# Top-1 experts: outputs scattered to their tokens by carried row numbers, loaded back in order

## The chip, the cores and the metric

The kernel runs as one program on 1 core of a Trainium2 chip. The metric is the device time of one execution in microseconds (us), lower is better. A core has five engines that run side by side and meet at semaphores: TensorE (PE; its weight loads are shown as PEld), VectorE (DVE), ScalarE (ACT), GpSimd (POOL) and SyncE (SP, used here to issue transfers). 16 DMA engines move data between DRAM and the on-chip memory SBUF. Two ways of issuing a transfer matter here: SP issues plain ones, whose rows stand as `SPq DMA_DIRECT2D`; POOL issues the indirect ones, whose addresses come from a table of row numbers in SBUF, and stands as busy for the `DMA_INDIRECT` while it does so.

## The reference

Four transformer-like layers of 4096 tokens by 128 channels run in sequence, each as "x = x + mixer(norm(x))" and "x = x + feed-forward(norm(x))". The change is in the feed-forward of the second layer (L1), a mixture of 8 experts:

```python
def _L1_ffn_ref(x, router_w, W1, b1, W2, b2):
    ...
    capacity = int(math.ceil(T / E * CAPACITY_FACTOR))      # 4096 / 8 * 1.25 = 640
    logits = tokens @ router_w.T
    # top-1 expert; the tokens of an expert beyond its capacity (by probability) go to expert 0
    final_e = _route(tokens, router_w)
    out = jnp.zeros_like(tokens)
    for e in range(E):
        h = jax.nn.relu(tokens @ W1[e] + b1[e])             # 128 -> 512
        y = h @ W2[e] + b2[e]                               # 512 -> 128
        out = out + jnp.where((final_e == e)[:, None], y, 0.0)
    return out.reshape(Lx, Bx, D)
```

The other layers (two attentions, two gated mixtures, two state-space mixers, a spiking network) are not touched.

## The kernel before, in words

`build` calls the stages one after the other; each stage is a block in which the five engines have their own instruction lists, and at its end all engines meet before the next begins. The activations stand transposed in SBUF (`g.xT`, channels by tokens). `P` is 128, `TOK` 4096, `NT` = 32 tiles of 128 tokens, `CH` 512 and `NCH` = 8 chunks. Around the change the order is: `norm_stage` n3, `top1_stage` (routing), `expert_stage`, `norm_stage` n4.

**Routing (`top1_stage`).** PE makes the logits (L771). DVE takes the first maximum and the probability, then searches each expert's capacity threshold in 28 bisection steps, each with a count that PE sums over the partitions (L1010). Meanwhile PE turns the tokens' rows back (L998) and ACT copies them to `routed.rows` (L1123), 128 floats for each token. After the search DVE works out for each token a slot (`routed.slot`, L1099): the slots are grouped by expert and padded to blocks of 256 slots, 23 blocks (`BLOCKS`), 5888 slots (`SLOTS`) in all. After it come nine more instructions of DVE (L1101 to L1115), one after the other: which expert owns which block (`routed.expert`), and the biases of each block (`routed.b1`, `routed.b2`). POOL clears a 128x128 tile (L984), and SP writes it over the whole table `sent` in DRAM (L989), so that empty slots hold zeros.

**Experts (`expert_stage`).** POOL's list in order: 32 indirect scatters, one for each tile of 128 tokens, from `routed.rows` to the slots in `sent` (L1158); for each block two copies of its expert's weights to a ring of three buffers (L1164, L1165), the fourth and later ones after the block three back has been through both its matmuls (`y_ready`); at last a wait for all stores, and 32 indirect gathers (L1169), one for each tile of tokens, from `back` at the tokens' slots. SP's list: after all scatters have landed, 8 loads of `sent`, three blocks each (L1176), the next stage's weights (L83), and for each block a store of its output rows to `back`, in slot order (L1181). PE runs a software pipeline over the blocks: `turn_x(i+1)` (L1191), `up(i)` (L1200), `down(i-1)` (L1209), `turn_y(i-2)` (L1218). ACT does the four ReLUs of a block (L1252) and the copy of its output rows `rows(i)` to the ring `yr` of three (L1245), three blocks behind. DVE copies the turned inputs (L1265) and adds the second bias (L1271). Behind the last block PE turns each gathered chunk of four tiles (L1236) and DVE adds it to `g.xT` (L1282).

Of the kernel before, what the change touches and what calls it, by code (L numbers as in the profile page):

```python
# [18 lines left out]
P = 128  # L19
# [921 lines left out]
SLOTS = BLOCKS * BLOCK  # L941

class Routed:

    def __init__(self, nc, ctx):
        make = lambda n, shape, dt=F32: ctx.enter_context(nc.sbuf_tensor("f1_" + n, shape, dt))
        self.rows, self.slot = make("rows", [P, NT, P]), make("slot", [P, NT], mybir.dt.int32)
        self.expert = make("expert", [P, BLOCKS], mybir.dt.int32)  # L950
        self.b1, self.b2 = make("b1c", [P, BLOCKS, 4]), make("b2c", [P, BLOCKS])
# [4 lines left out]
def top1_stage(nc, g, name, w, experts, routed):  # L956
# [5 lines left out]
    with Stage(nc, name) as s:  # L962
# [4 lines left out]
        zero = s.sb("zero", [P, P])  # L967
        count_k, block_k = s.sb("count_k", [P, BLOCKS]), s.sb("block_k", [P, BLOCKS])
        own = s.sb("own", [P, BLOCKS, e])
        need, ends, expert = s.sb("need", [P, e]), s.sb("last", [P, e]), s.sb("expert", [P, BLOCKS])  # L970
        over, b1m, b2m = s.sb("over", [P, e, 16]), s.sb("b1m", [P, BLOCKS, 4, e]), s.sb("b2m", [P, BLOCKS, e])
# [9 lines left out]
        with nc.Block() as block:  # L981
            @block.gpsimd
            def _(pool):
                pool.memset(zero[:, :], 0.0).then_inc(zeroed, 1)  # L984

            @block.sync
            def _(sp):
                sp.wait_ge(zeroed, 1)
                sp.dma_start(routed.sent.rearrange("(i p) d -> p i d", p=P),  # L989
                             zero[:, :].unsqueeze(1).to_broadcast([P, SLOTS // P, P])).then_inc(cleared, 16)  # L990
# [3 lines left out]
            def _(pe):  # L994
# [26 lines left out]
            def _(dve):  # L1021
# [19 lines left out]
                link(dve.tensor_tensor(pm[:, :, :], oh[:, :, :], p1[:, :].unsqueeze(2).to_broadcast(wide), ALU.mult))  # L1041
                link(dve.memset(thr[:, :], 0.0))
# [57 lines left out]
                per_block = lambda t: t.unsqueeze(2).to_broadcast([P, BLOCKS, e])  # L1100
                link(dve.tensor_tensor(own[:, :, :], per_block(block_k[:, :]),  # L1101
# [1117 lines left out]
```

## Time and profile before

| | |
|---|---|
| median of 3 runs | 3723.78 us (3715.41 to 3729.06) |
| the profiled execution's own time | 3735.14 us, span 3733.4 us |
| mean granted TensorE clock | 0.877 of full speed |
| busy share of the span: PE, DVE, ACT, POOL | 79%, 68%, 49%, 19% |
| routing stage, first to last work | 2159.2 to 2277.9 us |
| experts, 32 scatters on POOL | 2279.1 to 2319.3 us |
| experts, 23 blocks | 2324.0 to 2417.7 us |
| experts, 32 gathers, turns and adds | 2420.3 to 2463.5 us |
| norm stage n4 begins | 2465.6 us |

A row of a timeline reads: start, duration, engine, line, operation, output<-inputs, shapes, count, and in brackets how long the engine had been idle before it and what ended the idle time. A row of the windows reads: stretch, its length, then the busy time and number of instructions of PE, PEld, DVE, ACT and POOL, then the granted clock of TensorE (1.00 is 2.4 GHz, 0.50 is 1.2 GHz), the busy share of the DMA engines and the GB/s that they moved.

### The profile page before, as it was taken

To read this page: it belongs to the slowest core of one execution; us is meant where nothing else is said; L and a number is where in the kernel's file an instruction comes from. 1 tells how busy PE (TensorE), PEld (TensorE's weight loads), DVE (VectorE), ACT (ScalarE), POOL (GpSimd) and SP (SyncE) were. 2 spreads that over 40 slices of the span, in tenths; PEclk is the share of its full clock that TensorE was granted. 3 is DMA by queue.
4 is the path that set the end of the run, shared out by engine and by line. 5 is a ranking of instruction groups with operands and counts; after the bars stand their busy time and mean duration, and the time that the engine had idled before them with its cause. 6 is when DMAs were issued, how large, how long until landed. Compare 5 with 4: busy or idle time off the path is not lost. (4 is left out here: it accounts for less than half of the span.)

```text
span 3733.4 us, 43485 instructions
## 1 busy us (share of the span) xinstructions
PE 2943.2 (79%) x12844; PEld 1022.8 (27%) x12844; DVE 2552.6 (68%) x2898; ACT 1818.1 (49%) x3121; POOL 726.6 (19%) x820
## 2 busy tenths in 40 slices
PE   6499999975999948999999542856777786996756
PEld 3122222213333321222222131722223333332322
DVE  4699999923444459999997252147999984447448
ACT  2288888851212226888888300425655541224333
POOL 3311111100000031111110003223777760000000
PEclk8599999965999968999999655977999997998778
DMA  3210111002000040010100212110100000001010
GB/s 118 81 27 23 27 27 26 23 20 68 0 0 0 0 156 22 23 27 22 27 22 19 97 34 58 36 46 23 42 6 12 12 1 0 0 0 56 0 45 23
DMA packets 113619, 116.36 MB, mean 31 GB/s; under 512 B 37118, under 2 KB 89982, under 8 KB 113100
## 3 DMA queue, kind: packets, MB, share of 16 engines
q1 hardware_dynamic: 99148, 84.38, 7.6%
q0 software_dynamic: 14336, 30.44, 2.8%
q8 instruction: 53, 0.87, 0.1%
q14 instruction: 82, 0.67, 0.1%
HBM read 64.15 MB, written 50.59 MB: 31 GB/s over the span
## 5 line engine op out<-in xcount | busy, mean ns | idle before, releaser
L640 DVE TENSOR_REDUCE a_att_mx<-a_att_s 128x2 f32<-128x1024 f32 x1024 | 1205.3, 1220 | 104.1 <-PE a_att_s L551 91.9
L625 ACT ACTIVATE a_att_pt<-a_att_st 128x512 f32<-128x512 f32 x2048 | 1064.7, 602 | 283.0 <-PE a_att_st L577 265.0
L577 PE MATMUL a_att_st<-a_att_qst,a_att_kst 50*128 50x512 bf16 x2048 | 636.1, 394 | 75.4 <-ACT a_att_pt L625 62.7
L551 PE MATMUL a_att_s<-a_att_kst,a_att_qst 50*128 50x512 bf16 x2048 | 531.7, 402 | 83.9 <-DMA a_att_kst<-a_kstk 50.9
L564 PE MATMUL a_att_av<-a_att_pt,a_att_vst 128*32 128x512 f32 x4096 | 565.9, 626 | 0.0
L577 PEld LDWEIGHTS a_att_st<-a_att_qst,a_att_kst 50*128 50x128 bf16 x2048 | 158.3, 94 | 766.1 <-ACT a_att_pt L625 708.3
L929 DVE TENSOR_TENSOR f_h<-f_sg,f_up 128x512 f32<-128x512 f32 x184 | 126.6, 688 | 309.4 <-ACT f_sg L917 309.4
L917 ACT ACTIVATE f_sg<-f_gp 128x512 f32<-128x512 f32 x184 | 109.9, 597 | 461.2 <-PE f_cp L906 461.2
L1656 POOL TENSOR_TENSOR g_xn<-m2s_hs,m2s_cb 128x1024 f32<-128x1024 f32 x128 | 300.8, 2354 | 119.0 <-DVE m2s_hs L1623 62.2
L1623 DVE TENSOR_TENSOR_SCAN m2s_hs<-m2s_da,m2s_bps 128x1024 f32<-128x1024 f32 x128 | 292.7, 2287 | 4.4
L1539 PE MATMUL m2s_yps<-g_xn,g_ident 128*128 128x512 f32 x512 | 242.8, 597 | 0.9
L487 POOL CAST a_att_mt_in<-a_att_nmax 128x16 bf16<-128x16 f32 x64 | 12.6, 196 | 1081.3 <-DVE a_att_nmax L648 1081.3
L1595 ACT COPY m2s_cb<-m2s_cps 128x1024 f32<-128x1024 f32 x128 | 129.5, 1012 | 183.9 <-POOL g_xn L1656 182.4
L551 PEld LDWEIGHTS a_att_s<-a_att_kst,a_att_qst 50*128 50x128 bf16 x2048 | 113.4, 94 | 237.9 <-DVE a_att_mx L640 168.5
L163 POOL MEMSET n_mean_w<- 128x128 f32 x8 | 1.6, 204 | 898.6 <-POOLq L875 586.8
L1618 DVE TENSOR_TENSOR m2s_bps<-m2s_dtx,m2s_bps 128x1024 f32<-128x1024 f32 x128 | 154.8, 1209 | 3.8 <-POOL m2s_dtx L1642 3.8
L1590 ACT ACTIVATE m2s_da<-m_dt,m2s_aneg 128x1024 f32<-128x1024 f32 x128 | 147.4, 1151 | 0.0
L1559 PE MATMUL m2s_bps<-m_bcs,m2s_sel 96*128 96x512 bf16 x256 | 79.2, 392 | 85.5 <-DVE m2s_hs L1623 82.7
L931 DVE TENSOR_TENSOR f_h<-f_h,f_cp 128x512 f32<-128x512 f32 x184 | 126.4, 687 | 6.3
L896 PE MATMUL f_yp<-f_h,area 128*128 128x512 f32 x224 | 126.0, 645 | 4.3 <-DVE f_h L931 4.3
L270 ACT ACT_TABLE_LOAD x9 | 11.5, 1283 | 224.3 <-PEq L696 107.7
L1539 PEld LDWEIGHTS m2s_yps<-g_xn,g_ident 128*128 128x128 f32 x512 | 97.1, 191 | 85.2 <-issue 63.9
(387 smaller groups left out, 3590.1 us busy)
## 6 DMA issues: line engine op xcount, KB each, us to landing
a_att_qst<-a_qstk POOLq DMA_DIRECT2D x128, 100.0 KB, 2.5
a_att_kst<-a_kstk POOLq DMA_DIRECT2D x128, 100.0 KB, 2.5
a_qstk<-a_qkv_part SPq DMA_DIRECT2D x96, 128.0 KB, 1.9
a_kstk<-a_qkv_part SPq DMA_DIRECT2D x96, 128.0 KB, 2.0
a_num<-a_att_oev SPq DMA_DIRECT2D x256, 16.0 KB
a_out_nm<-a_num SPq DMA_DIRECT2D x16, 256.0 KB, 3.4
a_out_rb<-a_rden SPq DMA_DIRECT2D x16, 256.0 KB, 4.5
area<-in_f_w_dram SPq DMA_DIRECT2D x2, 2048.0 KB, 10.1
```

Of the source, the lines that this page charges most:

```text
L551: mm = pe.matmul(s1[:, cut % 2, h, :], qst[u][64 * h:64 * h + STACK, qt * P:(qt + 1) * P], kst[u][64 * h:64 * h + STACK, kh * CH:(kh + 1) ...
L564: mm = pe.matmul(av[32 * gr:32 * gr + 32, :], vst[u][:, kt, h, :], pt[:, 4 * (kt % 4) + 2 * half + h, :], start=kt == 0, stop=kt == 7)
L577: pe.matmul(st[:, e % 3, :], kst[u][64 * h:64 * h + STACK, kt * P:(kt + 1) * P], qst[u][64 * h:64 * h + STACK, half * CH:(half + 1) * CH], ...
L625: act.activation(pt[:, e % 16, :], st[:, e % 3, :], ACT.Exp, scale=scale).then_inc(exp_done, 1)
L640: dve.tensor_reduce(mx[:, par, 2 * cut:2 * cut + 2], s1[:, cut % 2, :, :], AX.X, ALU.max).then_inc(s1_used, 1)
L929: dve.tensor_tensor(h1[:, j % 2, :], sg[:, j % 2, :], up[:, j % 2, :], ALU.mult).then_inc(h1_done, 1)
L1539: mm = pe.matmul(yps[:, f, :], g.ident[:, :], hc[:, k % 4, f * CH:(f + 1) * CH], start=n == 0, stop=n == NS - 1)
L1590: act.activation(da[:, k % 4, :], dt[:, q % 2, span(q)], ACT.Exp, scale=aneg[:, q % 2, n:n + 1]).then_inc(da_done, 1)
L1595: act.copy(cb[:, k % 2, :], both(cps[:, :, :])).then_inc(c_copied, 1)
L1618: dve.tensor_tensor(over, dtx[:, q % 2, :], over, ALU.mult).then_inc(dbx_done, 1)
L1623: dve.tensor_tensor_scan(hs[:, k % 3, :], da[:, k % 4, :], over, 0.0, ALU.mult, ALU.add).then_inc(scan_done, 1)
L1656: pool.tensor_tensor(hc[:, k % 4, :], hs[:, k % 3, :], cb[:, k % 2, :], ALU.mult).then_inc(hc_done, 1)
```

## The change

The rows that travel get wider: 132 floats (`WIDE`) in place of 128, where the float at place 128 holds a number. For a token's row it is the token's own number; for every row of the cleared table it is 4096 plus the slot's number. So after the scatter each slot carries the row of `back` to which its output belongs, and `back` grows to 4096 + 5888 rows. In `top1_stage` this takes one matmul, five small DVE instructions ahead of the search, a larger memset on POOL (128x6072 in place of 128x128), and a clearing transfer that waits for the numbers. In `expert_stage` DVE turns the numbers of three blocks to integers at a time (`take_numbers`, 8 times), and POOL, for each block, issues two indirect scatters of its 256 output rows straight to their tokens' rows; SP then has no stores in the loop, and at the end loads the 4096 rows in order with 8 plain transfers. The 32 gathers are gone. The nine DVE instructions that make the blocks' experts and biases stand at the head of `expert_stage`; POOL's weight copies and ACT's first ReLU wait for them (`blocks_ready`). The weight ring has four buffers in place of three, and ACT's `rows` runs two blocks behind in place of three.

```diff
@@ Routed
-        self.rows, self.slot = make("rows", [P, NT, P]), make("slot", [P, NT], mybir.dt.int32)
+        self.rows, self.slot = make("rows", [P, NT, WIDE]), make("slot", [P, NT], mybir.dt.int32)
-        self.sent = nc.dram_tensor("f1_sent", [SLOTS, P], F32, kind="Internal").ap()
-        self.back = nc.dram_tensor("f1_back", [SLOTS, P], F32, kind="Internal").ap()
+        self.sent = nc.dram_tensor("f1_sent", [SLOTS, WIDE], F32, kind="Internal").ap()
+        self.back = nc.dram_tensor("f1_back", [TOK + SLOTS, P], F32, kind="Internal").ap()
@@ top1_stage, POOL and SP
-                pool.memset(zero[:, :], 0.0).then_inc(zeroed, 1)
+                pool.memset(empty[:, :, :], 0.0).then_inc(zeroed, 1)
+                pool.memset(routed.rows[:, :, P:WIDE], 0.0).then_inc(zeroed, 1)
-                sp.wait_ge(zeroed, 1)
-                sp.dma_start(routed.sent.rearrange("(i p) d -> p i d", p=P),
-                             zero[:, :].unsqueeze(1).to_broadcast([P, SLOTS // P, P])).then_inc(cleared, 16)
+                sp.wait_ge(zeroed, 2)
+                sp.wait_ge(numbered, 1)
+                sp.dma_start(routed.sent.rearrange("(i p) d -> p i d", p=P), empty[:, :, :]).then_inc(cleared, 16)
@@ top1_stage, PE (behind the logits) and DVE (ahead of the search)
+                pe.matmul(pre_ps[:, 0:1], before_w[:, :], g.ones[:, 0:1], start=True, stop=True).then_inc(place_ps_ready, 1)
+                dve.wait_ge(place_ps_ready, 1)
+                link(dve.tensor_scalar(serial[:, :], g.ones[:, 0:SLOTS // P], float(P), None, ALU.mult))
+                link(dve.tensor_tensor_scan(number[:, :], g.ones[:, 0:SLOTS // P], serial[:, :], -float(P), ALU.mult, ALU.add))
+                link(dve.tensor_tensor(number[:, :], number[:, :], pre_ps[:, 0:1].to_broadcast([P, SLOTS // P]), ALU.add))
+                dve.wait_ge(zeroed, 2)
+                link(dve.tensor_copy(routed.rows[:, :, P], number[:, 0:NT]))
+                dve.tensor_scalar(empty[:, :, P], number[:, :], float(TOK), None, ALU.add).then_inc(numbered, 1)
@@ top1_stage, DVE: L1100 to L1115 leave; they stand at the head of expert_stage's DVE list, the last with
+                dve.tensor_reduce(routed.b2[:, :], b2m[:, :, :], AX.X, ALU.add).then_inc(blocks_ready, 1)
+                dve.wait_ge(blocks_ready, 1)
@@ expert_stage, POOL
                 pool.wait_ge(w.here, w.all)
+                pool.wait_ge(blocks_ready, 1)
+
+                def take_weights(i):
+                    first = pool.value_load(routed.expert[0:1, i:i + 1], min_val=0, max_val=7) * CH
+                    if i >= 4:
+                        pool.wait_ge(y_ready, i - 3)
+                    pool.tensor_copy(wu[:, i % 4, :], w1[:, bass.ds(first, CH)]).then_inc(w_copied, 1)
+                    pool.tensor_copy(wd[:, i % 4, :], w2[:, bass.ds(first, CH)]).then_inc(w_copied, 1)
+
+                for i in range(4):
+                    take_weights(i)
                 for i in range(BLOCKS):
-                    first = pool.value_load(routed.expert[0:1, i:i + 1], min_val=0, max_val=7) * CH
-                    if i >= 3:
-                        pool.wait_ge(y_ready, i - 2)
-                    pool.tensor_copy(wu[:, i % 3, :], w1[:, bass.ds(first, CH)]).then_inc(w_copied, 1)
-                    pool.tensor_copy(wd[:, i % 3, :], w2[:, bass.ds(first, CH)]).then_inc(w_copied, 1)
-                for u in range(3):
-                    pool.wait_ge(r_stored[u], 16 * len(range(u, BLOCKS, 3)))
-                for t in range(NT):
-                    pool.indirect_dma_start(got[:, t, :], None, routed.back, place(t)).then_inc(gathered[t // 4], 16)
+                    if i + 4 < BLOCKS:
+                        take_weights(i + 4)
+                    if i % 3 == 0:
+                        pool.wait_ge(to_ready, i // 3 + 1)
+                    pool.wait_ge(r_copied, i + 1)
+                    for j in range(wide):
+                        pool.indirect_dma_start(routed.back, bass.IndirectOffsetOnAxis(
+                            ap=to[:, wide * i + j:wide * i + j + 1], axis=0), yr[:, i % 3, j, :], None).then_inc(r_sent[i % 3], 16)
@@ expert_stage, SP
-                for i in range(BLOCKS):
-                    sp.wait_ge(r_copied, i + 1)
-                    sp.dma_start(back[:, wide * i:wide * (i + 1), :], yr[:, i % 3, :, :]).then_inc(r_stored[i % 3], 16)
+                for u in range(3):
+                    sp.wait_ge(r_sent[u], 32 * len(range(u, BLOCKS, 3)))
+                for c in range(NCH):
+                    sp.dma_start(got[:, 4 * c:4 * c + 4, :], back[:, 4 * c:4 * c + 4, :]).then_inc(got_here[c], 16)
@@ expert_stage, PE
-                    pe.wait_ge(gathered[c], 64)
+                    pe.wait_ge(got_here[c], 16)
@@ expert_stage, ACT
-                        act.wait_ge(r_stored[i % 3], 16 * (i // 3))
+                        act.wait_ge(r_sent[i % 3], 32 * (i // 3))
+                act.wait_ge(blocks_ready, 1)
-                    if i >= 3:
-                        rows(i - 3)
-                for i in range(BLOCKS - 3, BLOCKS):
+                    if i >= 2:
+                        rows(i - 2)
+                for i in range(BLOCKS - 2, BLOCKS):
                     rows(i)
@@ expert_stage, DVE
+                def take_numbers(k):
+                    dve.wait_ge(x_here[k], 16)
+                    part = slice(wide * groups[k][0], wide * (groups[k][-1] + 1))
+                    dve.tensor_copy(to[:, part], xs[:, part, P]).then_inc(to_ready, 1)
+                    if i % 3 == 0 and i < BLOCKS:
+                        take_numbers(i // 3)
```

## Rows read from the trace of the kernel before

**Rows 1.** Windows of the expert stage and the norm stage behind it: busy time, clock, DMA share.

```profile
2320.60:2333.00 12.40, 8.95 (x36) 7.37 (x37) 2.04 (x5) 3.36 (x8) 2.72 (x6) 0.70 1.01 265
2332.00:2410.00 78.00, 78.00 (x402) 68.72 (x401) 17.30 (x41) 38.58 (x99) 23.38 (x40) 1.00 0.12 35
2426.60:2463.50 36.90, 8.93 (x32) 5.73 (x32) 5.50 (x8) 0.00 (x0) 25.47 (x27) 0.50 0.19 50
2465.50:2471.00 5.50, 5.18 (x6) 2.19 (x7) 1.38 (x2) 2.75 (x4) 1.09 (x2) 0.50 0.00 0
```

**Rows 2.** Timeline of VectorE at the end of the routing stage (start us, us).

```profile
2272.96 0.18 DVE L1099 CAST f_slot<-f1r_tmp 128x32 int32<-128x32 f32 x1
2273.17 0.35 DVE L1101 TENSOR_TENSOR f1r_own<-f1r_block_k,f1r_last 128x184 f32<-128x184 f32 x1
...
2274.75 1.41 DVE L1109 TENSOR_TENSOR f1r_b1m<-f1r_own,area 128x736 f32<-128x736 f32 x1
...
2277.53 0.34 DVE L1115 TENSOR_REDUCE f_b2c<-f1r_b2m 128x23 f32<-128x184 f32 x1
```

**Rows 3.** Timelines, VectorE and GpSimd: the nearest rows for the added small operations.

```profile
2178.59 0.18 DVE L1045 TENSOR_SCALAR f1r_count_k<-f1r_block_k 128x23 f32<-128x23 f32 x1
...
2134.61 0.95 POOL L164 MEMSET n_inv<- 128x1024 f32 x1
```

**Rows 4.** Timeline of GpSimd: first and last of 32 scatters, then the weight copies.

```profile
2279.09 1.06 POOL L1158 DMA_INDIRECT f_sent<-f_rows,f_slot  x1 [119.69 <-POOLq L981]
...
2318.34 0.96 POOL L1158 DMA_INDIRECT f_sent<-f_rows,f_slot  x1 [0.30 <-issue]
...
2319.31 0.62 POOL L1164 COPY f_wu<-area 128x512 f32 x1
```

**Rows 5.** One line's instructions: duration in ns, min/median/max, of the GpSimd DMAs.

```profile
L1158 POOL DMA_INDIRECT f_sent<-f_rows,f_slot x32: 954/958/1061, 2279.1 to 2318.3; - x32
...
L1169 POOL DMA_INDIRECT f_got<-f_back,f_slot x32: 940/944/1001, 2420.3 to 2459.1; - x32
...
L478 POOL DMA_DIRECT2D a_att_qst<-a_qstk x128: 518/518/738, 129.9 to 2005.4; - x128
```

**Rows 6.** Timeline of one block in the steady part of the block loop.

```profile
2367.18 0.61 POOL L1164 COPY f_wu<-area 128x512 f32 x1 [2.72 <-PE f_yp L1209]
...
2368.35 1.70 ACT L1252 ACTIVATE f_h<-f_zp,f_b1c 128x256 f32<-128x256 f32 x4 [1.93 <-PE f_zp L1200]
...
2370.74 0.38 PE L1218 MATMUL f_rp<-g_ident,f_y 128*128 128x128 f32 x2
```

**Rows 7.** Timeline from the last blocks to the first work of the next stage.

```profile
2413.76 0.37 ACT L1245 COPY f_yr<-f_rp 128x256 f32<-128x256 f32 x1 [0.84 <-PE f_rp L1218]
2417.31 0.37 ACT L1245 COPY f_yr<-f_rp 128x256 f32<-128x256 f32 x1 [0.59 <-PE f_rp L1218]
...
2420.30 1.00 POOL L1169 DMA_INDIRECT f_got<-f_back,f_slot  x1 [13.03 <-DMA f_back<-f_yr]
2426.67 1.11 PE L1236 MATMUL f_zp<-g_ident,f_got 128*128 128x128 f32 x4 [9.40 <-DMA f_got<-f_back,f_slot]
2462.79 0.69 DVE L1282 TENSOR_TENSOR g_xT<-g_xT,f_zp 128x512 f32<-128x512 f32 x1 [4.22 <-PE f_zp L1236]
2465.56 0.20 POOL L163 MEMSET n_mean_w<- 128x128 f32 x1 [5.55 <-POOLq L1153]
```

**Rows 8.** First loads; landing of the gathers, then of the clearing transfer; POOL's DMA queue.

```profile
2320.59 7.68 SPq L1176 DMA_DIRECT2D f_xs<-f_sent  x8
...
2323.96 1.12 PE L1191 MATMUL f_xp<-g_ident,f_xs 128*128 128x128 f32 x4 [56.26 <-DMA f_xs<-f_sent]
...
DMA to landing us min/median/max: 2.4/2.5/2.6
...
DMA to landing us min/median/max: 11.8/11.8/11.8
...
q0 software_dynamic: 2048, 4.20, 7.3%
```

More of the change, by code:

```diff
@@ L966, in top1_stage @@
         thr, cand, part, inc = (s.sb(x, [P, e]) for x in ("thr", "cand", "part", "inc"))
[L967 to L971, printed above, removed]
+        empty = s.sb("empty", [P, SLOTS // P, WIDE])
+        serial, number = s.sb("serial", [P, SLOTS // P]), s.sb("number", [P, SLOTS // P])
+        place_ps_ready, numbered = s.sem("place_ps_ready"), s.sem("numbered")
+        count_k = s.sb("count_k", [P, BLOCKS])
+        need, ends, block_k = s.sb("need", [P, e]), routed.ends, routed.block_k
+        over = s.sb("over", [P, e, 16])
         ps = s.ps("ps", [P, NT * e])
@@ L1099, in _ @@
                 link(dve.tensor_copy(routed.slot[:, :], tmp[:, :]))
-                per_block = lambda t: t.unsqueeze(2).to_broadcast([P, BLOCKS, e])
-                link(dve.tensor_tensor(own[:, :, :], per_block(block_k[:, :]),
-                                       ends[:, :].unsqueeze(1).to_broadcast([P, BLOCKS, e]), ALU.is_ge))
-                link(dve.tensor_reduce(expert[:, :], own[:, :, :], AX.X, ALU.add))
-                link(dve.tensor_scalar(expert[:, :], expert[:, :], float(e - 1), None, ALU.min))
-                link(dve.tensor_copy(routed.expert[:, :], expert[:, :]))
-                link(dve.tensor_tensor(own[:, :, :], per_block(expert[:, :]),
-                                       block_k[:, 0:e].unsqueeze(1).to_broadcast([P, BLOCKS, e]), ALU.is_equal))
-                dve.wait_ge(experts.here, experts.all)
-                link(dve.tensor_tensor(b1m[:, :, :, :], own[:, :, :].unsqueeze(2).to_broadcast([P, BLOCKS, 4, e]),
-                                       experts.tiles["b1"].rearrange("p (e t) -> p t e", t=4).unsqueeze(1).to_broadcast(
-                                           [P, BLOCKS, 4, e]), ALU.mult))
-                link(dve.tensor_reduce(routed.b1[:, :, :], b1m[:, :, :, :], AX.X, ALU.add))
-                link(dve.tensor_tensor(b2m[:, :, :], own[:, :, :],
-                                       experts.tiles["b2"].unsqueeze(1).to_broadcast([P, BLOCKS, e]), ALU.mult))
-                link(dve.tensor_reduce(routed.b2[:, :], b2m[:, :, :], AX.X, ALU.add))
             @block.scalar
@@ L1122, in _ @@
                     act.wait_ge(turned, c + 1)
-                    act.copy(routed.rows[:, 4 * c:4 * c + 4, :],
+                    act.copy(routed.rows[:, 4 * c:4 * c + 4, 0:P],
                              tps[:, c % 4, :].rearrange("p (t d) -> p t d", d=P)).then_inc(copied, 1)
@@ L1137, in expert_stage @@
         got = s.sb("got", [P, NT, P])
-        wu, wd = s.sb("wu", [P, 3, CH]), s.sb("wd", [P, 3, CH])
+        own, expert = s.sb("own", [P, BLOCKS, 8]), s.sb("number", [P, BLOCKS])
+        b1m, b2m = s.sb("b1m", [P, BLOCKS, 4, 8]), s.sb("b2m", [P, BLOCKS, 8])
+        step, blocks_ready = s.sem("step"), s.sem("blocks_ready")
+        wu, wd = s.sb("wu", [P, 4, CH]), s.sb("wd", [P, 4, CH])
         w_copied = s.sem("w_copied")
@@ L1146, in expert_stage @@
         r_turned, r_copied = s.sem("r_turned"), s.sem("r_copied")
-        r_stored = [s.sem(f"r_stored{u}") for u in range(3)]
-        gathered = [kept(f"gathered{c}") for c in range(NCH)]
+        to_ready, r_sent = s.sem("to_ready"), [kept(f"r_sent{u}") for u in range(3)]
+        got_here = [s.sem(f"got_here{c}") for c in range(NCH)]
         o_turned, o_added = s.sem("o_turned"), s.sem("o_added")
         sent = routed.sent.rearrange("(i p) d -> p i d", p=P)
-        back = routed.back.rearrange("(i p) d -> p i d", p=P)
+        back = routed.back[0:TOK, :].rearrange("(t p) d -> p t d", p=P)
         at = lambda i: (slice((i % 2) * BLOCK, (i % 2 + 1) * BLOCK))
```

34 lines of the change are left out of this document (28 added, 6 removed).

## The prediction

> **What bounds the kernel now.** The kernel is a chain of stages that do not overlap, so I first cut the expert stage into stretches and ask of each what ends it. I read four views: the windows, to see which engine fills a stretch; the timelines of VectorE and GpSimd, to see what stands alone; the durations of the GpSimd transfers; and the timeline of the last blocks. The windows [rows 1] show two quite different halves. In the block loop TensorE is busy 78.00 of 78 us at a granted clock of 1.00, so no other engine's work costs anything there as long as it fits under TensorE. From 2426.6 to 2463.5 us TensorE is busy 8.9 of 36.9 us, VectorE 5.5, and GpSimd 25.5: here the 32 gathers are the path. GpSimd's timeline [rows 4] shows that the 32 scatters in front are a path of the same kind: from 2279.09 to 2318.34 us is 31 steps, 1.266 us each, 0.96 of it the instruction and 0.30 the idle time before it. Between the routing's last instruction and the first scatter VectorE runs nine instructions on which the scatters do not depend [rows 2].
>
> **The change, part by part.**
>
> *The routing's end.* The slots are ready at 2272.96 + 0.18. The nine instructions from 2273.17 to 2277.53 + 0.34 leave the path: −4.70 us. They run beside the scatters instead, which take 40 us, and who waits for them (the weight copies, the first ReLU) comes behind the scatters; their cover is eight times their size. If the cover failed, the price is the same 4.7 us.
>
> *The numbers, ahead of the search.* Five small VectorE instructions on 46 or 32 columns. The nearest row is the 0.18 us one on 23 columns [rows 3]; with the gap to the next in the chain I take 0.24 us, 1.2 us together. Bounds are 1.0 and, by the 0.35 us of the 184 columns in [rows 2], 1.9 us. The extra matmul stands behind the logits, and TensorE's next wait there is on VectorE's first count, behind the same five instructions: nothing. GpSimd's memset grows to 6072 columns: by 0.95 us for 1024 [rows 3] 5.6 us, from 2159 to 2165; VectorE asks for it at 2178 (the row of L1045 is what now follows these instructions): nothing. The clearing transfer starts at about 2180 instead of 2160 and landed 11.8 us after its issue (the second landing line of [rows 8]); the stage ends 80 us later: nothing.
>
> *The 32 scatters with wider rows.* 528 bytes a row for 512. The queue moved 4.20 MB in 2048 packets [rows 8]: 64 indirect transfers of 128 rows are 8192 rows, so four rows of 512 bytes to a packet, and no sign of a limit at one row's size. The count of rows is unchanged; I take 1.266 us as before. Bounds: nothing, and 3.3 us if each took the slowest of 1061 ns [rows 5].
>
> *The first load.* It landed 3.4 us after its issue (2320.59 to 2323.96) [rows 8]; 3% more bytes are nothing. The four weight copies in front of the loop (4.5 us by two of some 0.6 each) end at about 2323.8, but the first block's pair is done at 2320.4: nothing. 
> *The block loop.* The period is 2.72 us idle plus two copies, 3.89 us [rows 6]. GpSimd gets two scatters for each block: 2 x 1.26 = 2.52, with the copies 1.17, together 3.69 us of 3.89. It fits by 0.2 us, which is thin, so I also ask what happens if it does not. The scatters are behind everything TensorE needs: the weight ring of four and the row ring of three give TensorE more than 3 us of lag before it stalls. What counts is the end of GpSimd's chain. The first rows are ready near 2336.3 (2414.13 less 20 periods); from there 46 scatters and 18 pairs of copies are 58.0 + 21.1 us, to 2415.4, while the rows of the last block are only ready at 2417.68. So in the loop nothing is lost. ACT's `rows(i-2)` now waits for the `turn_y` of the same round, which ends at 2370.74 + 0.38 = 2371.12; the copy takes 0.37 us [rows 7], to about 2371.6, and the next ReLU starts a period after 2368.35, at 2372.24 [rows 6]: 0.6 us of room, nothing. Its wait for `r_sent` is for rows scattered three periods (11.7 us) ago; those need 2.5 us of issue and 2.5 to land: nothing. The eight number casts are about 0.2 us of VectorE, which is busy 17.3 of 78 us: nothing.
>
> *The end.* Before, from the last rows at 2417.31 + 0.37 = 2417.68 to the last add's end at 2462.79 + 0.69 = 2463.48: 45.8 us [rows 7]. After, by steps. Block 20's rows are ready at 2413.76 + 0.37 = 2414.13; three blocks of scatters follow back to back, 7.6 us, to 2421.7. The last one lands 2.5 us after its start at 2420.7 (the landing that the gathers show, 2.4 to 2.6 [rows 8]): 2423.2. The first plain load, 256 KB against the 384 KB that took 3.4 us: 2.9 us, and 0.1 for the issue: 2426.2. The eight chunks: the loads come at 265 GB/s [rows 1], 1.0 us each, and TensorE turns a chunk in 1.11 us at a clock of 0.50 [rows 7], so TensorE sets the pace: 8 x 1.12 = 9.0, to 2435.2. The last add: 0.7 us, 2435.9. That is 18.2 us in place of 45.8: −27.6 us. The bounds: if the clock rises in the dense turns the loads pace them, −1.0; and n4, whose first 5.5 us ran at 0.50 [rows 1], could start at full clock, at most half of that, −2.7. The other way, a slower landing and loads without overlap with the turns: +3.
>
> *Sum.* −4.7 + 1.2 − 27.6 = −31.1 us. Against the profiled execution's own 3735.14 us it gives 3704.0; that execution was 11.4 us above the median, and I take the same difference from the median: 3723.78 − 31.1 = **3692.7 us**, 0.8% less. What this measurement can tell from no change is about 0.5%, 18.6 us.
>
> **The rivals.**
>
> *VectorE holds up the scatters (−26 to −29 us).* Nine instructions now run while GpSimd writes its transfers. In the profile the scatters ran while VectorE was idle. For the rival: nothing measured beside it. Against: attention's GpSimd transfers, made while every engine works, keep 518 ns in the median of 128, 738 at worst [rows 5], and the 32 gathers, beside the turns and adds, stayed at 940 to 1001 ns [rows 5]. Its price is at most the nine instructions, 4.7 us, giving 3697.4. The Trainium skill ("SBUF — State Buffer", Summary: rules for kernel authors) says that a VectorE instruction that uses both its ports, or has two SBUF inputs against a GpSimd one that reads SBUF, fully blocks the other. By it the two-input instructions (1.41 [rows 2] and three of some 0.35) and two small copies could cost up to 2.8 us, 3695.5; inside the loop VectorE reads PSUM, and that page has no block there.
>
> *GpSimd becomes the bound of the loop (slower than before).* In the loop the scatters would have to take longer than alone. The chain has 6.3 us of room (2415.4 to 2421.7). At 1.5 us a scatter the chain is 46 x 0.24 = 11.0 us longer, and the end moves by 4.7: 3697.4. The gain is gone when one takes 1.26 + (6.3 + 31.1)/46 = 2.07 us, 64% more; at 2.5 us the kernel is 20 us slower, 3743. For it: 3.69 of 3.89 us is thin, and no indirect transfer of the profile ran beside a busy TensorE and ScalarE. Against: the attention rows above, and the worst of 32 scatters at 1.06.
>
> *The wider row costs a second piece (no change).* If 528 bytes were issued as 512 and 16, the instruction's 0.96 us could double: 32 x 0.96 = 30.7 us, and the sum is −0.4: 3723. The packets of four rows speak against it.
>
> *The end is longer than thought (−20 to −26 us).* Eight loads behind a wait for 46 scattered writes, whose landing to DRAM rows spread at random no row shows; with 3 us more for landing and 4 for loads one after the other, 3700.
>
> **Chances and range.** Forecast, −28 to −36 us: 0.66. A smaller gain by one of the rivals above, −19 to −28: 0.22. Nothing left, by the second piece or by both thin places: 0.07. GpSimd as the bound and slower: 0.05. Faster by over 0.5%: 0.88, within: 0.07, slower: 0.05. The low end: −31.1 − 3.7 for the clock, less 5 for the scatter of medians of few runs, 3684. The high end: −31.1 + 4.7 + 3.3 + 0.7 = −22.4, and 5 for the same: 3706. What lies beyond is 0.15.
>
> **What would show it.** After: no `DMA_INDIRECT` that writes `got`; VectorE's block work between the first and fourth scatter; the stage's first scatter 3.5 us closer to the routing's start; 32 scatters in 40 us; a TensorE busy all through 23 periods of 3.89 us; the last output scatter 4 us behind the last copy of rows; and 18 us from there to the last add. Wrong it would be if scatters in the loop take over 1.4 us, if the period of the loop leaves 3.89, if the first 32 stretch, or if the eight loads come much slower than 1.1 us apiece.

## The result, and the profile after

The changed kernel took 3687.4 us in the median of six executions, the kernel before 3724.56 us in six beside them: a ratio of 0.9887, 95% interval [0.9866, 0.9908]. On 3724.6 us that is 42 us less, between 34 and 50. Timed twice more beside the kernel before, the same file came out at 0.9901 [0.9877, 0.9925] and 0.9914 [0.9887, 0.9940]. The mean of all 24 executions is 3688.7 us, that of the 81 of the kernel before 3725.2 us: 36.5 us less, 1.0%. Forecast were 31.1 us less and a range from 3684 to 3706. The six executions' median lies inside it; the first ratio, taken of the 3723.78 us from which the range was worked out, gives 3681.7 us, 2 us below it.

The profiled execution took 3684.66 us, its span is 3683.3 us. Laid beside the profile before, by stages (us; the norm stages' starts are GpSimd's memset of L163):

| stretch | before | after | change |
|---|---|---|---|
| first norm stage to second (first attention, untouched) | 861.6 | 842.9 | −18.7 |
| second norm stage to routing (untouched) | 1284.1 | 1283.6 | −0.5 |
| routing, to the first input scatter | 119.9 | 116.2 | −3.7 |
| first input scatter to last | 39.25 | 40.10 | +0.85 |
| last input scatter to first turn of a block | 5.6 | 5.8 | +0.2 |
| first turn to last rows | 93.7 | 94.9 | +1.2 |
| last rows to last add | 45.8 | 16.8 | −29.0 |
| last add to next stage | 2.1 | 0.5 | −1.6 |
| norm stage n4 | 24.7 | 21.9 | −2.8 |
| n4's end to the end (untouched) | 1243.1 | 1247.0 | +3.9 |

The touched stages and n4 give 34.8 us. What else differs lies in code that the change does not touch, and there is a theory to test.

Windows of the changed kernel (stretch, length, busy time of PE, PEld, DVE, ACT, POOL, then the granted clock, DMA share and GB/s):

```profile
2298.70:2311.00 12.30, 8.66 (x28) 6.97 (x29) 1.28 (x4) 3.35 (x8) 3.12 (x6) 0.60 1.07 272
2311.00:2389.00 78.00, 78.00 (x401) 68.75 (x401) 17.69 (x47) 40.59 (x99) 58.79 (x76) 1.00 0.10 33
...
2414.40:2420.00 5.60, 5.31 (x12) 2.20 (x12) 3.43 (x5) 4.01 (x6) 1.09 (x2) 1.00 0.00 0
```

These answer to [rows 1]. TensorE is again busy 78.00 of 78 us in the loop, and GpSimd there went from 23.4 to 58.8 us without costing TensorE anything. In the last row n4's first 5.6 us run at a clock of 1.00; before it was 0.50.

The timelines of VectorE and of GpSimd around the stage's start, to lay beside [rows 2, 4]:

```profile
2254.87 0.18 DVE L1112 CAST f_slot<-f1r_tmp 128x32 int32<-128x32 f32 x1
2255.56 0.35 DVE L1282 TENSOR_TENSOR f_own<-f_block_k,f_ends 128x184 f32<-128x184 f32 x1 [0.51 <-PEq L985]
...
2256.75 0.35 DVE L1287 TENSOR_TENSOR f_own<-f_number,f_block_k 128x184 f32<-128x184 f32 x1
2257.14 1.42 DVE L1290 TENSOR_TENSOR f_b1m<-f_own,area 128x736 f32<-128x736 f32 x1
2258.59 0.92 DVE L1293 TENSOR_REDUCE f_b1c<-f_b1m 128x92 f32<-128x736 f32 x1
```

```profile
2256.28 1.05 POOL L1158 DMA_INDIRECT f_sent<-f_rows,f_slot  x1 [110.92 <-POOLq L985]
2257.63 1.78 POOL L1158 DMA_INDIRECT f_sent<-f_rows,f_slot  x1 [0.30 <-issue]
2259.72 1.00 POOL L1158 DMA_INDIRECT f_sent<-f_rows,f_slot  x1 [0.30 <-issue]
...
2296.38 0.95 POOL L1158 DMA_INDIRECT f_sent<-f_rows,f_slot  x1 [0.30 <-issue]
```

The slots are ready at 2255.05, the block work stands at 2255.56 behind the stage's switch, and the first scatter issues 1.2 us behind the slots. The second scatter takes 1.78 us in place of 0.96. It starts 0.5 us into VectorE's 1.42 us instruction with two inputs and ends 0.85 us behind it. The first, with the 0.35 us two-input instruction at 2256.75 wholly inside it, takes 1.05 us, as before (1.06).

GpSimd in the steady loop, the first scatter of four blocks in a row, with the number cast and the copy of rows that the fourth of them needs:

```profile
2362.83 0.16 DVE L1315 CAST f_to<-f_xs 128x6 int32<-128x6 f32 x1
2363.40 0.97 POOL L1178 DMA_INDIRECT f_back<-f_yr,f_to  x1 [0.97 <-DVE f_to L1315]
...
2366.98 0.97 POOL L1178 DMA_INDIRECT f_back<-f_yr,f_to  x1 [0.17 <-issue]
...
2370.71 0.96 POOL L1178 DMA_INDIRECT f_back<-f_yr,f_to  x1 [0.33 <-ACT f_yr L1256]
...
2373.95 0.37 ACT L1256 COPY f_yr<-f_rp 128x256 f32<-128x256 f32 x1 [1.11 <-PE f_rp L1229]
2375.08 0.96 POOL L1178 DMA_INDIRECT f_back<-f_yr,f_to  x1 [0.97 <-DVE f_to L1315]
```

Three blocks in 11.68 us, 3.893 each: TensorE's period. From 2363.40 to 2366.98 GpSimd runs free, at 3.58 us a block; then it catches up with the rows and waits for them, 0.33 us and 0.97 us. The profile puts the 0.97 us down to a number cast, but the cast that this block needs had ended 12 us before. The block waits for its rows too: they stood at 2374.32, and it starts 0.76 us behind them, where the block before starts 0.28 us behind its own. Why each third block, the one that also asks for its numbers, starts later is not shown. GpSimd's scatters take 954/963/972 ns (min/median/max of 46).

The end, to lay beside [rows 7]:

```profile
2396.75 0.37 ACT L1256 COPY f_yr<-f_rp 128x256 f32<-128x256 f32 x1 [0.59 <-PE f_rp L1229]
...
2400.70 0.96 POOL L1178 DMA_INDIRECT f_back<-f_yr,f_to  x1 [0.30 <-issue]
2402.98 5.37 SPq L1192 DMA_DIRECT2D f_got<-f_back  x8
...
2405.90 1.97 PE L1247 MATMUL f_zp<-g_ident,f_got 128*128 128x128 f32 x8 [9.19 <-DMA f_got<-f_back]
...
2410.38 3.54 DVE L1327 TENSOR_TENSOR g_xT<-g_xT,f_zp 128x512 f32<-128x512 f32 x5 [0.18 <-PE f_zp L1247]
...
2414.43 0.20 POOL L163 MEMSET n_mean_w<- 128x128 f32 x1 [12.78 <-POOLq L1153]
```

The last scatter ends 4.5 us behind the last rows, the loads issue 1.3 us later, the first turn comes 2.9 us behind the issue, and the last add ends 8.0 us after that, at 2413.92. The steps forecast were 4.0, 1.6, 2.9 and 9.7. The first is 0.5 us longer because the last three blocks do not follow back to back: block 21's rows stood at 2396.15, and its first scatter began at 2396.91.

### The profile page after: what moved, and what is told of

It is laid out like the page before. It is cut to its first block and busy times, and to the rows that moved or that the text cites. A ratio compares the mean times of both kernels' runs of the same rounds, so it can differ in the third digit from the quotient of the medians.

```text
span 3683.3 us, 43526 instructions
## 1 busy us (share of the span) xinstructions
PE 2919.2 (79%) x12846; PEld 1023.0 (28%) x12846; DVE 2553.5 (69%) x2911; ACT 1819.9 (49%) x3121; POOL 746.6 (20%) x835
## 5 line engine op out<-in xcount | busy, mean ns | idle before, releaser
L564 PE MATMUL a_att_av<-a_att_pt,a_att_vst 128*32 128x512 f32 x4096 | 554.1, 614 | 0.0
L163 POOL MEMSET n_mean_w<- 128x128 f32 x8 | 1.6, 204 | 896.8 <-POOLq L875 586.5
L904 PE MATMUL f_gp<-g_xn,area 128*128 x224 | 115.8, 599 | 4.3 <-POOL f_sel L884 4.3
```

The source lines that it names most:

```text
L564: mm = pe.matmul(av[32 * gr:32 * gr + 32, :], vst[u][:, kt, h, :], pt[:, 4 * (kt % 4) + 2 * half + h, :], start=kt == 0, stop=kt == 7)
```

## The experiments

**Is the part outside the stages real?** The kernel before against itself, and the changed kernel twice more. No edit.

> The kernel before, unchanged, timed against itself. Theory A (the 19 us by which the first attention was shorter in the profile after, with no edit in it, are the scatter of single executions): a ratio of 1.000 with an interval of some 0.003, and a first attention (from the first norm stage's start at 13.5 us to the second's) that lies anywhere from 843 to 862 us. Rival B (something in the changed program makes the untouched stages faster): the first attention again at 862 us here.

Measured: ratio 1.0003 [0.9982, 1.0023], twelve executions from 3712 to 3744. Its timeline has the norm stages' starts here:

```profile
13.64 0.20 POOL L163 MEMSET n_mean_w<- 128x128 f32 x1 [10.66 <-POOLq L101]
...
858.16 0.20 POOL L163 MEMSET n_mean_w<- 128x128 f32 x1 [93.40 <-POOLq L696]
```

and the changed kernel's is

```profile
13.65 0.20 POOL L163 MEMSET n_mean_w<- 128x128 f32 x1 [10.77 <-POOLq L101]
...
856.50 0.20 POOL L163 MEMSET n_mean_w<- 128x128 f32 x1 [92.95 <-POOLq L696]
```

The kernel before can do the first attention in 844.5 us too. Over the 15 profiles of this study it took 841 to 845 us in eight and 861 us in five, two times 852, in kernels of both kinds; the second attention took 845 to 848 us in thirteen and 864 to 865 in two. The length changes from one execution of the same file to the next. Theory A holds.

The traces also show where the 18 us lie. The end of the first attention in the profile before, in `before_warm`, in this run and in the changed kernel:

```profile
770.00:800.00 30.00, 27.20 (x102) 3.57 (x99) 0.00 (x0) 17.51 (x34) 0.00 (x0) 0.52 0.03 5
770.00:800.00 30.00, 25.66 (x129) 4.62 (x129) 0.00 (x0) 22.64 (x44) 0.00 (x0) 0.78 0.02 3
770.00:800.00 30.00, 23.61 (x150) 5.50 (x153) 0.00 (x0) 26.40 (x52) 0.00 (x0) 1.00 0.02 4
770.00:800.00 30.00, 24.09 (x157) 5.41 (x153) 0.00 (x0) 26.12 (x51) 0.00 (x0) 1.00 0.02 3
```

It is TensorE's granted clock: 1.00 in this stretch in the eight short ones, 0.50 to 0.52 in the five long ones, 0.78 and 0.79 in the two of 852 us. The two long second attentions have 0.69 in a stretch of 30 us near their end where the thirteen others have 1.00. From 760 to 770 us the clock stood at 1.00 with TensorE busy 8.40 of 10 us, in the profile before and in this run alike; then it fell in the one and not in the other. What made it fall is not shown.

> The changed kernel, unchanged, once more. Stage by stage the change should be worth 32.0 us from the routing's start to the next norm stage's and 2.8 us in that norm stage, 34.8 us or a ratio of 0.9907. Theory A: the ratio comes out at 0.990 to 0.992, and the first attention differs from the 842.9 us of the other profile. Rival B: the ratio is again 0.9887 or below, and the first attention is near 843 us.

Measured: 0.9901 [0.9877, 0.9925]; routing's start to n4's 275.4 us, n4 22.0, first attention 843.1. The stages gave 33.7 us this time. The ratio could be of either theory, so:

> The changed kernel a third time, unchanged. Theory A (the untouched attention stages have two lengths some 18 us apart, drawn anew in each execution, so that medians of few runs scatter by several us about the 34.8 us that the stages show): ratio between 0.989 and 0.993, nearer to 0.9907 than the first 0.9887. Rival B (a gain of some 7 us outside the stages that the change touches): 0.9885 or below.

Measured: 0.9914 [0.9887, 0.9940]; stages 275.2 and 21.0 us, 34.9 us less than before. By the ratio the gain outside did not come back. The three ratios centre on 0.9901, the stages say 0.9907.

**The block work undone.** L1100 to L1115 stand again at the end of the routing, and the waits for `blocks_ready` are gone:

```diff
@@ top1_stage, DVE
                 link(dve.tensor_copy(routed.slot[:, :], tmp[:, :]))
+                link(dve.tensor_tensor(own[:, :, :], per_block(block_k[:, :]), ...))
...
+                link(dve.tensor_reduce(routed.b2[:, :], b2m[:, :, :], AX.X, ALU.add))
@@ expert_stage, POOL and ACT
-                pool.wait_ge(blocks_ready, 1)
-                act.wait_ge(blocks_ready, 1)
```

> The changed kernel with one part undone: the nine VectorE instructions that make the blocks' experts and biases are back at the end of the routing, ahead of the scatters. The prediction's step (4.7 us off the path) says that from the routing's start to the next norm stage it takes 4.7 us more than the change as made, less the 0.8 us by which the second scatter was longer beside them, so 3.9 us more, and that the 32 scatters are back at 40.2 us. Rival (the move is worth nothing, since the scatters or the stage's switch hide it): 0 to 1 us more.

Measured: ratio 0.9915 [0.9890, 0.9940]. Routing to the first scatter took 121.1 us in place of 116.2, the scatters 39.24 in place of 40.10, and routing to n4 279.4 us: 4.0 to 5.1 us more than the changed kernel's three profiles (274.4 to 275.4). The second scatter took 0.97 us again. The step is right, with the long scatter as its price.

**More load on GpSimd in the loop.**

```diff
+                    for j in range(1):    # 2 in the second kernel; the waits on r_sent count them
+                        pool.indirect_dma_start(routed.spare, bass.IndirectOffsetOnAxis(
+                            ap=to[:, wide * i + j:wide * i + j + 1], axis=0), yr[:, i % 3, j, :], None).then_inc(r_sent[i % 3], 16)
```

> The changed kernel with one more indirect scatter per block in the loop, to a table that nobody reads (three in place of two); the output is unchanged. In the changed kernel's trace GpSimd's free period is 3.57 us (two scatters, two copies) under TensorE's 3.89. Theory (the prediction's chain: nothing is lost until GpSimd's chain is longer than TensorE's, and then its length counts alone): the period becomes 4.83 us for the 18 steps with a weight copy and 3.79 for the last four, the last scatter ends 105.7 us after the first in place of 85.0, and routing to next norm takes 20.7 us more than the change as made. Rival (TensorE stalls for weights or rows on top, and the two delays add): more than 25 us.

> The same with two more scatters per block (four in place of two). Theory: 6.09 us a block, 134.6 us from first to last, 49.6 us more than the change as made: slower than the kernel before by 15. The step from one extra to two is 23 x 1.26 = 29 us, each scatter at its full price once GpSimd is the bound. Rival (stalls add): more than 55 us.

Measured, routing to n4: 293.7 us with one more (19.3 us more than the changed kernel, forecast 20.7) and 324.1 us with two (49.8, forecast 49.6). The steady loop with one more:

```profile
2361.16 0.97 POOL L1179 DMA_INDIRECT f_back<-f_yr,f_to  x1 [0.17 <-issue]
...
2363.71 0.96 POOL L1182 DMA_INDIRECT f_spare<-f_yr,f_to  x1 [0.30 <-issue]
...
2366.01 0.97 POOL L1179 DMA_INDIRECT f_back<-f_yr,f_to  x1 [0.17 <-issue]
```

4.85 us a block and no wait but GpSimd's own issue. The two executions took 3705.7 and 3740.8 us. From the first output scatter to the end of the last it is 85.0 us in the changed kernel, 105.7 with one more a block and 134.7 with two, where 85.0, 105.7 and 134.6 were forecast. So the chain that the prediction used is the right model: the margin is spent first, about 8 us of it over the loop (23 x 1.26 less 20.7), and then each scatter costs its full 1.26 us, 23 times. Stalls of TensorE add nothing that shows. (The 1.4 us by which the first kernel came out below its forecast lie ahead of the chain: its first rows stood 12.4 us behind the first turn, the changed kernel's 13.8, with a clock of 1.00 against 0.70 in the second four us.)

**The scatters, but not under the loop.**

```diff
-y, yr = s.sb("y", [P, 2, BLOCK]), s.sb("yr", [P, 3, wide, P])
+y, yr = s.sb("y", [P, 2, BLOCK]), s.sb("yr", [P, BLOCKS, wide, P])
@@ POOL
+                for i in range(BLOCKS):
...
-                    pool.wait_ge(r_copied, i + 1)
+                    pool.wait_ge(r_copied, BLOCKS)
@@ ACT, rows(i)
-                        act.wait_ge(r_sent[i % 3], 32 * (i // 3))
```

> The changed kernel with the output scatters not block by block: GpSimd waits for the last block's rows and issues all 46 then, from a row buffer of 23 blocks. The output is unchanged. Theory (the change gains because the indirect transfers lie under TensorE's block loop; by themselves they are dearer than the 32 gathers): 46 x 1.266 = 58.2 us behind the last rows at about 2397.2, 53.8 us more than the change as made, about 19 us slower than the kernel before: ratio 1.005. Rival (it gains because plain loads in order replaced the gathers, whatever the place of the scatters): at most 10 us more than the change as made.

Measured: ratio 1.0022 [1.0007, 1.0038], slower than before. First and last of the 46:

```profile
2394.67 0.97 POOL L1179 DMA_INDIRECT f_back<-f_yr,f_to  x1 [15.06 <-ACT f_yr L1255]
...
2451.49 0.95 POOL L1179 DMA_INDIRECT f_back<-f_yr,f_to  x1 [0.30 <-issue]
```

56.8 us from start to start, 1.263 us each, and routing to n4 took 328.7 us: 54.3 more than the change as made. With n4's clock it is 19 us more than before by the stages; the ratio says 3 to 14. The direction is clear, the size is not the same in both. (The lowest of its ten executions, 3729.9 us, lies 20 us above the lowest of the 81 of the kernel before, 3709.9, which fits the stages.) Plain ordered loads alone do not make the gain. 46 scatters are dearer than 32 gathers, and they pay because they lie under TensorE.

**n4 and the clock.** Matmuls that nobody reads keep TensorE at work during the gathers of the kernel before:

```diff
+                def warm(n):
+                    for _ in range(n):
+                        pe.matmul(xp[:, 0, :], g.ones[:, :], g.xn[:, 0:CH], start=True, stop=True)
+
+                warm(8)                       # 10 in the second kernel
                 for c in range(NCH):
                     pe.wait_ge(gathered[c], 64)
...
                     mm.then_inc(o_turned, 1)
+                    if c < NCH - 1:
+                        warm(3)               # second kernel: 4, and 2 behind the last chunk
```

> The kernel before, with extra matmuls on TensorE whose result nobody reads: eight of 512 columns behind the block loop, and three behind each turned chunk but the last, so that TensorE stays busy while the gathers run. The output is unchanged. Theory (the 2.8 us that the norm stage behind gains come from TensorE's clock, which was still at 2.4 GHz when it began): the gathers take as long as before, the norm stage begins at a clock of 1.00 and takes 21.9 us in place of 24.7; 2.8 us faster in all, ratio 0.9992. Rival (the norm stage gains from something else in the change): it still takes 24.7 us.

Measured: ratio 0.9988 [0.9971, 1.0005], n4 24.6 us. It missed its condition, as the windows show, the second of them n4's start:

```profile
2420.00:2442.00 22.00, 13.03 (x41) 5.90 (x42) 2.75 (x4) 0.00 (x0) 16.51 (x19) 1.00 0.19 51
2450.73:2456.23 5.50, 5.24 (x6) 2.18 (x7) 1.38 (x2) 2.75 (x4) 1.09 (x2) 0.50 0.02 3
```

> The first such run missed its own condition: the clock had fallen to 0.50 before the norm stage began. Now the kernel before has ten extra matmuls of 512 columns behind the block loop, four behind each turned chunk and two behind the last. Theory (the 2.8 us of the norm stage are TensorE's clock): if the norm stage begins at a clock of 1.00 it takes 21.9 us in place of 24.7. Rival (it gains from something else): 24.7 us at a clock of 1.00.

Measured: the last extra matmul ended at 2442.45, TensorE then had 1.9 us without work, and n4 began at 2444.05 with a clock that fell in its first microseconds:

```profile
2442.00:2444.00 2.00, 0.45 (x2) 0.00 (x0) 0.00 (x0) 0.00 (x0) 0.00 (x0) 1.00 0.00 0
2444.05:2449.55 5.50, 5.24 (x9) 2.22 (x10) 2.04 (x3) 2.74 (x4) 1.09 (x2) 0.69 0.00 0
```

It took 23.7 us (the one execution, 3712.6). The condition was met by half, and so was the gain. Ordered by the mean clock of n4's first 5.5 us, over the 15 profiles: 0.50, 24.6 to 24.7 us (three profiles, all with gathers); 0.69, 23.7; 1.00, 21.0 to 22.0 (eleven). The length follows the clock, also within the kernel with the gathers. I take the term as TensorE's clock, shown in direction and, from one half-way point, in size.

**VectorE beside the input scatters.** Sixteen instructions that nobody needs, behind the block work:

```diff
                 dve.wait_ge(blocks_ready, 1)
+                for _ in range(16):
+                    link(dve.tensor_copy(got[:, 0:16, :].rearrange("p t d -> p (t d)"), g.xn[:, 0:2048]))
+                    # second kernel: dve.tensor_tensor(same, g.xn[:, 0:2048], g.xn[:, 2048:4096], ALU.add)
```

> The changed kernel with 16 more VectorE copies of 128x2048 float32 from SBUF to SBUF beside the 32 input scatters, behind the nine block instructions; nobody reads what they write. In the changed kernel the second of the 32 scatters took 1.78 us in place of 0.96, beside the 1.42 us two-input instruction and the two small copies. Theory A (the Trainium skill, SBUF page: a VectorE copy in a two-port mode and a GpSimd instruction exclude each other, descriptor writing too): the scatters beside the copies take up to a copy's length more each, and the 32 take 5 to 20 us more than 40.1. Rival B (the long scatter was of the two-input instruction's making or of chance): 40.1 us, and no scatter over 1.1 us but the one.

> The same with 16 VectorE additions of two SBUF inputs, 128x2048 float32 each, some 2.1 us apiece. Theory A (two SBUF inputs exclude a GpSimd instruction that reads SBUF; whether descriptor writing is one is what the page leaves as inferred): if it does, the scatters beside them stretch by 5 to 30 us in all; if only the two-port copies do, they stay at 40.1 us with one long one at the start. By the changed kernel's trace, where the long scatter lies under the 1.42 us two-input instruction, I expect them to stretch.

Measured, first input scatter to last: 50.1 us with the copies, 57.5 us with the additions, against 40.1. (The one execution of each took 3726.4 and 3694.1 us; both attentions were long in the first and neither in the second, so the totals say nothing of the scatters.) The copies (one merged row of 16) and one scatter beside and one behind them:

```profile
2295.28 20.37 DVE L1299 COPY f_got<-g_xn 128x2048 f32<-128x2048 f32 x16
...
2303.45 2.22 POOL L1158 DMA_INDIRECT f_sent<-f_rows,f_slot  x1 [0.30 <-issue]
...
2316.07 0.96 POOL L1158 DMA_INDIRECT f_sent<-f_rows,f_slot  x1 [0.31 <-issue]
```

and the additions with the same:

```profile
2256.51 37.19 DVE L1299 TENSOR_TENSOR f_got<-g_xn 128x2048 f32<-128x2048 f32 x16
...
2280.87 2.03 POOL L1158 DMA_INDIRECT f_sent<-f_rows,f_slot  x1 [0.30 <-issue]
...
2294.83 0.96 POOL L1158 DMA_INDIRECT f_sent<-f_rows,f_slot  x1 [0.30 <-issue]
```

**What the profile pointed to further.** TensorE starts the block loop at a clock of 0.60 (the first window of the changed kernel, shown above) and the search runs at 0.50. Extra matmuls in front of the loop, and in the second kernel in each step of the search too:

```diff
@@ expert_stage, PE (POOL counts its first 26 scatters on a semaphore of their own)
+                pe.wait_ge(early, 16 * 26)
+                for _ in range(8):
+                    pe.matmul(zp[:, 0, :], g.ones[:, :], g.xn[:, 0:CH], start=True, stop=True)
                 turn_x(0)
@@ top1_stage, PE, each step of the search (second kernel only)
                     turn(k + 3)
+                    for _ in range(2):
+                        pe.matmul(tot_ps[:, 0:256], g.ones[:, :], g.xn[:, 0:256], start=True, stop=True)
                     pe.wait_ge(counted_here, k + 1)
```

> The changed kernel with eight matmuls of 512 columns on TensorE, whose result nobody reads, placed so that they run while the last six input scatters go out (a semaphore of its own for the first 26). Theory (the first blocks ran at a clock of 0.50 after 47 us without work; the changed kernel still has this): the block loop starts at 1.00, the first three blocks take some 3 us less, from routing to next norm 271 us in place of 274.4; ratio to the kernel before 0.990. Rival (the clock falls again before the first block, or the loop's first steps wait for loads anyway): nothing.

> The same, and in each of the 29 steps of the threshold search two more matmuls of 256 columns on TensorE ahead of its wait for VectorE's count. Theory: at a clock of 1.00 the count that VectorE waits 0.69 us for each time comes about 0.2 us sooner, 29 times: the routing takes 110 to 112 us in place of 116.2, and with the 3 us above the whole is some 8 us faster than the changed kernel, ratio 0.988. Rival (the clock does not hold between so few columns, or the extra matmuls delay the count): 116 us or more.

Measured by stages: routing to n4 272.4 us with the first edit and 268.4 us with both, against 274.4 to 275.4: 2 to 3 and 6 to 7 us less (forecast were 3, and some 8). In the second the routing took 113.0 us for 110 to 112 forecast, the clock stood at 0.66 in the search and not at 1.00, and the loop began at 1.00:

```profile
2145.00:2252.00 107.00, 74.08 (x257) 52.52 (x257) 61.93 (x229) 4.99 (x9) 0.11 (x1) 0.66 0.12 29
2296.00:2304.00 8.00, 5.62 (x27) 4.21 (x26) 1.26 (x4) 2.80 (x7) 2.31 (x5) 1.00 1.10 282
```

The ratios are 0.9888 [0.9859, 0.9918] and 0.9907 [0.9874, 0.9939] (with one execution of 8436 us apart from the rest), which cannot be told from the changed kernel's. By stages the second is the fastest version here, 6 to 7 us ahead of the changed kernel and 4 ahead of the first edit; by the timing that is not shown.

## Why the prediction was off, point by point

The mechanism was right and the sum came close, 31.1 us for the 34.8 that the stages show; the low end of the range was wrong. The step that failed is the range's: "less 5 for the scatter of medians of few runs". The attention stages change by 18 us from one execution to the next, in both kernels, with TensorE's granted clock, and a ratio of six to twelve executions moves by more than 5 us: the same file gave 0.9887, 0.9901 and 0.9914, that is 42, 37 and 32 us less. The first lies 7 us beyond the 34.8 us of the stages, which alone would give 3689 us, inside the range. The three times shown spread by 13.6 us, and that could have been read as more than 5 on a median. The profile before held a sign too: the end of its first attention ran at a clock of 0.52 (shown above), and the end of its second, the same lines of the kernel, at 1.00:

```profile
2036.68:2066.68 30.00, 24.16 (x157) 5.57 (x153) 4.60 (x6) 26.46 (x52) 0.41 (x2) 1.00 0.04 7
```

The sum was 3.7 us short of the stages' gain. It had no term for the stage's switch (1.6 us), and it left n4's clock (2.8 us) out as a bound.

The terms, forecast and measured in the first profile:

- *The routing's end*, −4.7 + 1.2 = −3.5: −3.7, and the undoing of the move cost 4 to 5 us. Right.
- *The numbers, the clearing transfer, the memset*: the five instructions took 1.1 us (forecast 1.2), the rest nothing, as said; the memset took 5.16 us (forecast 5.6).
- *The scatters with wider rows*: 0.96 us as before. The second piece for 528 bytes, and with it the rival of no change, is gone.
- *VectorE holds up the scatters*: this rival came true at a sixth of its bound, +0.85 us. The evidence used against it did not bear on it: attention's transfers, which are plain ones, ran beside reductions, and the gathers beside adds of which one input is PSUM. Neither made them longer.
- *The first load*: 5.8 us from the last scatter to the first turn against 5.6. The Trainium skill's rule ("DMA: Bandwidth & Descriptors", How a descriptor splits into AXI transactions), by which the prediction estimated 0.4 us, is neither borne out nor refuted: no run here tells 0.4 from this 0.2.
- *The block loop*: no loss to GpSimd, as said, with 3.58 us free a block (forecast 3.69). From the first turn to the last rows it took 1.2 us more, at a clock of 0.60 where before it was 0.70 in the stretch around the first blocks; this was not forecast. Over the profiles without extra scatters this length, too, follows the clock. It is 93.4 to 93.8 us where the clock was 0.97 to 1.00 between 4 and 8 us behind the first turn (the kernels with gathers, and `dve_copy`), 94.8 to 94.9 where it was 0.70 to 0.74 there (the changed kernel, `bias_back`, `at_end`, `dve_tt`), and 92.2 where it was 1.00 from the first turn on (`warm_head`, `warm_all`).
- *The end*: −27.6 forecast, −29.0 measured, and −28.2 and −28.1 in the changed kernel's two other profiles. From the first turn to the last add it was 8.0, 8.9 and 8.9 us for 9.7 forecast. In the first profile the clock reached 1.00 at about 2411.4, as the bound allowed; in the others it stayed at 0.50 to 0.58. The 0.8 us that all three gained is not the clock's: two chunks turned in 1.97 us at 0.50, where the prediction took 1.12 for each from a chunk that was turned alone. The chain of scatters in front gave 0.5 us of it back.
- *The stage's switch*: no term at all, and it gave 1.6 us. Before, GpSimd began the next stage 5.55 us after its last gather had been issued, also in the kernel with extra matmuls (`before_warm2`):

```profile
2440.77 0.69 DVE L1288 TENSOR_TENSOR g_xT<-g_xT,f_zp 128x512 f32<-128x512 f32 x1 [4.29 <-PE f_zp L1241]
...
2444.05 0.20 POOL L163 MEMSET n_mean_w<- 128x128 f32 x1 [5.55 <-POOLq L1153]
```

  VectorE's last add ended at 2441.46 here, 2.6 us ahead of the next stage, and in the kernel before 2.1 us ahead; the stage's switch takes 0.5 us where nothing else is late, as after. So GpSimd was the last to leave the stage, 1.6 us behind the add in the kernel before and 2.1 us in this one. That its last gathers hold it is an inference: 5.55 us recurs in all four profiles with gathers at the end.
- *n4*: the prediction had it as a bound, −2.7, and left it out of the sum. It was −2.7 to −3.7 in the changed kernel's profiles, −2.8 in the first. With this and the switch in the sum it would have been −35.5, against −34.8 measured.
- *GpSimd as the bound of the loop*: the forecast's break-even model held in both kernels that loaded it, 19.3 for 20.7 and 49.8 for 49.6.

What stays open: `at_end` is 19 us slower by stages and 8 by the ratio. Executions with long or short attentions would explain that much, but no run separates it. And what makes TensorE's clock fall near the end of an attention in some executions was not found.

## What to carry to other kernels

When an indirect transfer costs an engine 1.26 us for each 128 rows, ask where that engine is idle under another one's bound, and let a number travel with each row so that the scatter can be issued there; compare GpSimd's chain with TensorE's from the first rows on, not one block with another. When a wait at a stage's end goes, look at what the idle had cost the next stage, in clock above all. And read the spread of times first: a change of 1% in a kernel whose untouched stages jump by 18 us is measured in its stages, not in six executions; the granted clock of each stretch says where a stage jumps.

## What the runs showed of the hardware

- 128x2048 float32 VectorE additions with both inputs in SBUF doubled an indirect transfer's issue on GpSimd (0.96 to 2.02 us), and SBUF to SBUF copies of that size did too (2.22 us). A two-input instruction of 0.35 us inside a scatter cost nothing that shows. Gathers beside adds from PSUM stayed at 0.94 to 1.00 us, plain transfers beside reductions at 0.52.
- GpSimd began the next stage 5.55 us behind the issue of its last indirect gather in all four profiles with gathers there, whatever the other engines did.
- The first attention stage, untouched, takes about 843 or 861 us by the execution, with a granted clock of 1.00 or 0.50 in one and the same stretch near its end.
- Indirect scatters of 512-byte rows land 2.2 us after their issue (median of 46), 2.3 us with 528-byte rows; spread at random over DRAM rows they are no slower than gathers (2.5 us).
